# Attentions 0 and 2 of a four-layer cross-attention kernel: reciprocal, head sum and small TensorE pieces placed elsewhere in a half

## Chip, cores and metric

The kernel runs on one core of a Trainium2 chip. The metric is the time of one execution on the device in microseconds (us), as a median over runs.

## The reference

Four layers follow each other, and each adds a cross-attention and a feed-forward part to `x` (32 batches of 56 rows of 128 values). All four attentions look at the same context `ctx_768` (32 x 1500 x 96). Attentions 0 and 2 have 16 heads of 8 values:

```python
q = (einsum('bld,ed->ble', layernorm(x), Wq) + bq) -> (b, 56, 16, 8)
k, v = projections of ctx_768                       -> (b, 1500, 16, 8)
att = softmax(q . k / sqrt(8), over the 1500 keys)
x = x + (att . v) @ Wo + bo
```

Attention 2 has no biases and takes a mask of the keys. Attention 1 (heads of 64), attention 3 (one head) and the feed-forward parts are written by other code, which the change leaves alone.

## The kernel before

Everything is float32, the products of the projections in part as a high and a low float32r piece. Attentions 0 and 2 run `attend_turned`, each engine with a program of its own, tied by semaphores. The batches go in pairs. A pair is worked in four **halves** (h = 0 to 3; 64 halves for the 16 pairs): half h of pair i is batch 2i + h // 2 and heads 8 (h % 2) onwards. `pairs` writes out the halves at both ends and loops over those between. An order written out by hand decides everything: `half` of TensorE has twelve slots k = 0 to 11, and in slot k it issues

- `turned_scores`: two matmuls of scores with the keys on the partitions, into one of three PSUM buffers (`ring`); ScalarE's `exps` makes probabilities of them (`prob_t`). The order of uses of `ring` stands in `turns` (T is a slot, X the projection of a part of the keys or values), and each use waits for the reader of the use three before it;
- `scores`: one matmul of scores with the queries on the partitions for the half after the next one, into one of three banks (`ps_s`); VectorE's `maxima` takes their row maximum. Scores k waits for maximum k - 3.

Between the slots stand the smaller pieces: `keys` (odd halves, k = 0, 2, 4), whose result ScalarE's `high_keys` and VectorE's `low_keys` split into `k_hi` and `k_lo`, which the SyncE queue then copies into `ks` for the scores (`spread_keys`, six DMAs, eight with the mask row); `values` (even halves, k = 2, 4, 6); `products` (probabilities times values, three groups per half, two of them at k = 1 of the next half); `shifts` (turns the maxima, for `keep_shifts` on ScalarE); `queries`; `project`; and `denominators`, whose result VectorE's `invert` takes the reciprocal of. GpSimd picks queries by head (`pick_queries`), masks the sums by head (`own_rows`) and multiplies by the reciprocal (`quotient`). `ps_m` is one PSUM bank that shifts, queries, projection and denominators share in turn, so each waits for the reader of the one before.

The ring's order of use, for even and odd halves:

```python
turns = ("T0 T1 T2 X0 T3 T4 X1 T5 T6 X2 T7 T8 T9 T10 T11", "T0 X0 T1 T2 X1 T3 T4 X2 T5 T6 T7 T8 T9 T10 T11")
```

Of the kernel before, what the change touches and what calls it, by code (L numbers as in the profile page):

```python
# [29 lines left out]
ALU = mybir.AluOpType  # L30
ACT = mybir.ActivationFunctionType
AX = mybir.AxisListType
# [289 lines left out]
def attend_turned(nc, g, name, ctx_t, masked, ob, wk, wq3, bq3, wv, wo6):  # L322
# [16 lines left out]
    with ExitStack() as ctx:  # L339
# [21 lines left out]
         picked, scored, maxed, combined, max_high, max_split, shift_made, shifted, turned, exped, summed, o_kept,  # L361
         den_made, inverted, own_made, reduced, av_made, projected, out_kept) = (st.sem(x) for x in (
             "prepared", "filled", "k_made", "high_made", "k_kept", "v_made", "v_kept", "q_made", "q_biased",
             "q_rounded", "q_split", "picked", "scored", "maxed", "combined", "max_high", "max_split", "shift_made",
             "shifted", "turned", "exped", "summed", "o_kept", "den_made", "inverted", "own_made", "reduced",
             "av_made", "projected", "out_kept"))
# [10 lines left out]
        def asks(i, h):  # L377

            return h == (1 if isinstance(i, int) and i < 0 else 0) and among(i + 1, NP)
# [63 lines left out]
        def _(pool):  # L443
            def own_rows(m, b):

                pool.wait_ge(o_kept, m + 1)
                if up(m):
# [5 lines left out]
                    ALU.mult).then_inc(own_made, 1)  # L453

            def low_queries(i, h):

                pool.wait_ge(q_rounded, i + 2)
                if h == 0 and up(4 * i):
                    pool.wait_ge(own_made, 4 * i)
                low = slice(2 * qd, 3 * qd)  # L460
                pool.tensor_tensor(qp[low, :], qf[low, :], qp[low, :].bitcast(F32), ALU.subtract).then_inc(q_split, 1)
# [26 lines left out]
            def half(i, h):  # L488
# [5 lines left out]
                if among(m - 1, halves):  # L494
                    own_rows(m - 1, (h - 1) % 2)
                if asks(i, h):
                    low_queries(i, h)
# [13 lines left out]
        def _(pe):  # L511
# [145 lines left out]
            def half(i, h):  # L657
# [4 lines left out]
                for k in range(KT):  # L662
# [6 lines left out]
                    if k == 1 and behind:  # L669
                        products(m - 1, 2 * i + h // 2 - (1 - hf), (h - 1) % 4 // 2, (h - 1) % 2, 1)  # L670
                        products(m - 1, 2 * i + h // 2 - (1 - hf), (h - 1) % 4 // 2, (h - 1) % 2, 2)
                    if k == 1 and among(m + 1, halves):
                        shifts(i, h)
                    if x_live and not hf and k in (2, 4, 6):
                        values(i, h, k // 2 - 1)
                    if k == 5 and asks(i, h):
                        queries(i)
                    if k == (6 if hf else 7) and live:
                        products(m, n, h // 2, hf, 0)
                    if k == 7 and h == 1 and up(i):  # L680
                        project(i)
                    if k == 9 and behind:
                        denominators(i, h)
# [5 lines left out]
        def _(dve):  # L689
# [25 lines left out]

            def maxima(i, h, u):

                w = 4 * i + h + 2
                for c in range(BANKS):
                    dve.wait_ge(scored, 12 * w + 3 * u + c + 1)  # L720
                    dve.tensor_reduce(bank_max[:, h % 2, u, c:c + 1], ps_s[0:ur, c, 0:BK], AX.X, ALU.max  # L721
                                      ).then_inc(maxed, 1)

# [20 lines left out]

            def sum_heads(m):

                dve.wait_ge(own_made, m + 1)
                if up(m):
                    dve.wait_ge(av_made, m)
                dve.tensor_reduce(av_sum[:].rearrange("p (x l) -> p x l", x=groups),  # L750
                                  own_o[:].rearrange("p (x h l) -> p x l h", x=groups, h=3), AX.X, ALU.add
                                  ).then_inc(reduced, 1)

            def half(i, h):
                m, n, hf = 4 * i + h, 2 * i + h // 2, h % 2
                live, max_live = among(m - 1, halves), among(m + 2, halves)
                x_live = hf and among(n + 2, total)

                def unit(u):
                    if max_live:  # L760
                        maxima(i, h, u)

                if among(m - 2, halves):
                    invert(m - 2)
                if x_live:
                    low_keys(i, h, 0)
                unit(0)
                if x_live:
                    low_keys(i, h, 1)
                unit(1)  # L770
                if x_live:
                    low_keys(i, h, 2)
                if asks(i, h):
                    queries(i)
                if live:
                    sum_heads(m - 1)
                unit(2)
                unit(3)
                if max_live:
                    row_shifts(i, h)  # L780
# [26 lines left out]
        def _(act):  # L807
# [55 lines left out]
            def half(i, h):  # L863
# [11 lines left out]

                for k in range(7):
                    exps_of(k)
                    if k in ((0, 2, 4) if hf else (2, 4, 6)):
                        extra(k // 2 - (0 if hf else 1))
                    if k == 1 and among(m - 1, halves):  # L880
                        keep_sums(m - 1, (h - 1) % 2)
                    if k == 2 and among(m + 1, halves):
                        keep_shifts(i, h)
                if h == 1 and up(i):
                    out(i)
                exps_of(7, 8, 9, 10, 11)

# [1482 lines left out]
```

## Time and profile before

| | us |
|---|---|
| median of 3 runs | 5119.68 (5119.68 to 5135.09) |
| the profiled execution | 5126.65, its span 5125.0 |
| attention 0, first to last window | 204 to 1135 |
| attention 2 | 3660 to 4560 |
| rows of the page: PE, DVE, ACT, POOL busy | 4333.7, 3398.1, 2291.1, 1103.7 |

PE is TensorE's matmuls, DVE VectorE, ACT ScalarE, POOL GpSimd, SPq the DMA queue that SyncE issues. A row of a timeline is a run of like instructions: where it starts, how long it lasts, what it is, and in brackets how long its engine was idle ahead of it and for whom. Matmuls are pipelined, so the start of the next row, and not the length, tells what a piece costs.

### The profile page before, as it was taken

Reading aid. Unit: us, or ns where it says so; the run is one execution under the profiler, and the core shown is the slowest. Engines: PE = TensorE matmul, PEld = TensorE weight load, DVE = VectorE, ACT = ScalarE, POOL = GpSimd, SP = SyncE. Lnnn points to the kernel's source line nnn. Section 1 sums busy time; section 2 is a strip of 40 time slices with the busy share of each in tenths; the row PEclk is TensorE's granted clock in tenths of the full one; section 3 lists DMA queues with packets and bytes.
Section 4 is the critical chain, followed back from the end, with each engine's and each line's share of the span. In section 5 each row is a group of like instructions: output and inputs, shape, how many; then the busy total and the mean of one; then the engine's idle time right before and its main releaser. Section 6 shows DMA issues by size and latency. Waiting matters only on the chain. (4 is left out here: it accounts for less than half of the span.)

```text
span 5125.0 us, 100217 instructions
## 1 busy us (share of the span) xinstructions
PE 4333.7 (85%) x34185; PEld 3681.2 (72%) x34185; DVE 3398.1 (66%) x6401; ACT 2291.1 (45%) x4584; POOL 1103.7 (22%) x918
## 2 busy tenths in 40 slices
PE   5499999985599999999999667788699999969684
PEld 4277777764599899999999655566477777756573
DVE  4477777865666666665665466677677777755545
ACT  0066666652133333333333244465266666644341
POOL 0112221212101111111111044565122212213320
PEclk6599999987799999999999877888699999978897
DMA  7344445420101101101101100000245445410382
GB/s 244 91 109 108 102 105 112 103 47 10 46 19 33 24 19 33 24 19 33 24 19 24 43 25 0 0 0 0 64 108 113 103 101 113 108 30 16 71 181 46
DMA packets 190680, 316.83 MB, mean 62 GB/s; under 512 B 132372, under 2 KB 140870, under 8 KB 190406
## 3 DMA queue, kind: packets, MB, share of 16 engines
q1 hardware_dynamic: 186822, 294.71, 25.7%
q10 hardware_dynamic: 3584, 18.43, 0.9%
q8 instruction: 175, 2.87, 0.3%
q14 instruction: 99, 0.81, 0.1%
HBM read 146.07 MB, written 19.54 MB: 32 GB/s over the span
## 5 line engine op out<-in xcount | busy, mean ns | idle before, releaser
L1383 ACT ACTIVATE a1m_prob<-a1m_ps_s,a1m_neg_max 128x500 f32<-128x500 f32 x672 | 405.8, 675 | 588.7 <-DVE a1m_neg_max L1319 588.7
L1238 PE MATMUL a1m_ps_o<-a1m_cn,a1m_prob_t 125*128 125x97 f32 x5376 | 638.3, 276 | 0.2 <-issue 0.2
L1238 PEld LDWEIGHTS a1m_ps_o<-a1m_cn,a1m_prob_t 125*128 125x128 f32 x5376 | 624.7, 194 | 0.4 <-issue 0.4
L721 DVE TENSOR_REDUCE a0m_bank_max<-a0m_ps_s 112x1 f32<-112x500 f32 x768 | 486.7, 669 | 145.7 <-PE a0m_ps_s L583 140.6
L721 DVE TENSOR_REDUCE a2m_bank_max<-a2m_ps_s 112x1 f32<-112x500 f32 x768 | 486.4, 669 | 145.4 <-PE a2m_ps_s L583 140.5
L1316 DVE TENSOR_REDUCE a1m_bank_max<-a1m_ps_s 128x1 f32<-128x500 f32 x672 | 455.4, 678 | 174.1 <-PE a1m_ps_s L1204 172.7
L1204 PE MATMUL a1m_ps_s<-a1m_cxt,a1m_qhi 98*128 98x500 f32 x1344 | 442.3, 411 | 22.2 <-issue 18.1
L814 ACT ACTIVATE a0m_prob_t<-a0m_ring 125x448 f32<-125x448 f32 x768 | 385.9, 545 | 122.5 <-PE a0m_ring L537 115.3
L814 ACT ACTIVATE a2m_prob_t<-a2m_ring 125x448 f32<-125x448 f32 x768 | 386.0, 546 | 119.1 <-PE a2m_ring L537 111.7
L1220 PE MATMUL a1m_ps_t<-g_ident,a1m_prob 128*125 128x128 f32 x2688 | 378.2, 277 | 5.4 <-issue 4.3
L1220 PEld LDWEIGHTS a1m_ps_t<-g_ident,a1m_prob 128*125 128x125 f32 x2688 | 350.6, 190 | 26.4 <-issue 7.6
L1166 POOL TENSOR_TENSOR a1m_cxt<-a1m_raw,g_zeros 98x1500 fp32r<-98x1500 f32 x32 | 86.1, 2690 | 1297.3 <-PE a1m_ps_s L1204 1250.4
L537 PE MATMUL a0m_ring<-a0m_qs,a0m_ks 99*125 99x224 f32 x1536 | 357.0, 315 | 3.0 <-ACT a0m_prob_t L814 2.6
L537 PE MATMUL a2m_ring<-a2m_qs,a2m_ks 99*125 99x224 f32 x1536 | 355.8, 314 | 3.4 <-ACT a2m_prob_t L814 2.9
L583 PE MATMUL a2m_ps_s<-a2m_ks,a2m_qs 97*112 97x500 f32 x768 | 311.2, 409 | 23.5 <-DMA a2m_ks<-ctx_t 18.4
L583 PE MATMUL a0m_ps_s<-a0m_ks,a0m_qs 96*112 96x500 f32 x768 | 310.7, 408 | 22.9 <-DMA a0m_ks<-a0m_k_hi 17.9
L537 PEld LDWEIGHTS a0m_ring<-a0m_qs,a0m_ks 99*125 99x125 f32 x1536 | 264.7, 190 | 79.7 <-issue 35.4
L537 PEld LDWEIGHTS a2m_ring<-a2m_qs,a2m_ks 99*125 99x125 f32 x1536 | 264.0, 189 | 79.8 <-issue 35.2
L1327 DVE COPY a1m_prob_t<-a1m_ps_t 125x512 f32<-125x512 f32 x448 | 289.0, 686 | 8.0 <-PE a1m_ps_t L1220 7.0
L1391 ACT ACTIVATE a1m_prob_t<-a1m_ps_t 125x512 f32<-125x512 f32 x224 | 133.8, 597 | 357.1 <-PE a1m_ps_t L1220 357.1
L1204 PEld LDWEIGHTS a1m_ps_s<-a1m_cxt,a1m_qhi 98*128 98x128 f32 x1344 | 241.1, 193 | 59.8 <-issue 21.9
L1335 DVE RECIPROCAL a1m_den<-a1m_ps_o 128x1 f32<-128x1 f32 x224 | 37.7, 168 | 359.0 <-PE a1m_ps_o L1238 359.0
(783 smaller groups left out, 9138.8 us busy)
## 6 DMA issues: line engine op xcount, KB each, us to landing
a0m_ks<-a0m_k_hi SPq DMA_DIRECT2D x256, 187.5 KB
a2m_ks<-a2m_k_hi SPq DMA_DIRECT2D x256, 187.5 KB
a0m_ks<-a0m_k_lo SPq DMA_DIRECT2D x128, 187.5 KB
a2m_ks<-a2m_k_lo SPq DMA_DIRECT2D x128, 187.5 KB
ctx_t<-cprep_tr ACTq DMA_DIRECT2D x32, 562.5 KB
a0m_raw<-ctx_t SPq DMA_DIRECT2D x32, 562.5 KB
a1m_raw<-ctx_t SPq DMA_DIRECT2D x32, 562.5 KB
a2m_raw<-ctx_t SPq DMA_DIRECT2D x32, 562.5 KB
```

What stands on the lines that cost most here:

```text
L537: r = pe.matmul(out[0:NK, q * hr // 2:(q + 1) * hr // 2], ks[0:kt, b, x, k * NK:(k + 1) * NK], qs[0:kt, b, x * hr // 2:(x + 1) * hr // 2], ...
L583: r = pe.matmul(ps_s[0:ur, c, 0:BK], qs[0:kr, b, at:at + ur], ks[0:kr, b, x, c * BK:(c + 1) * BK], start=True, stop=True)
L721: dve.tensor_reduce(bank_max[:, h % 2, u, c:c + 1], ps_s[0:ur, c, 0:BK], AX.X, ALU.max).then_inc(maxed, 1)
L814: act.activation(prob_t[:, k // 4, k % 4, :], ring[where[h % 2, "T", k] % 3][0:NK, 0:hr], ACT.Exp).then_inc(exped, 1)
L1166: pool.tensor_tensor(cxt[:, h, 0, :], raw[:, h, :], g.zeros[0:CR, 0:1].broadcast_to([CR, S]), ALU.add).then_inc(high_made[h], 1)
L1204: m = pe.matmul(ps_s[:, k, 0:BK], part[:, b, h, at], cxt[:, h, w, keys], start=(part is qhi and w == 0 and h == sequences(u)[0]), stop=(pa ...
L1220: m = pe.transpose(ps_t[(BANKS * u + k) % 2][0:NK, q * P:(q + 1) * P], prob[:, u % 2, t * NK:(t + 1) * NK], g.ident[:])
L1238: m = pe.matmul(ps_o[at, 0:CO], prob_t[:, u % 2, t, at], cn[:, h, t, :], start=(t == 0), stop=(t == KT - 1))
L1316: dve.tensor_reduce(bank_max[:, s, k:k + 1], ps_s[:, k, 0:BK], AX.X, ALU.max).then_inc(bank_maxed, 1)
L1327: dve.tensor_copy(prob_t[:, u % 2, k * GT:(k + 1) * GT, :], ps_t[(BANKS * u + k) % 2][0:NK, :].rearrange("p (t r) -> p t r", t=GT)).then_i ...
L1383: act.activation(prob[:, s, k * BK:(k + 1) * BK], ps_s[:, k, 0:BK], ACT.Exp, bias=neg_max[:, s:s + 1]).then_inc(exped, 1)
L1391: act.activation(prob_t[:, u % 2, 2 * GT:KT, :], ps_t[(BANKS * u + 2) % 2][0:NK, :].rearrange("p (t r) -> p t r", t=GT), ACT.Copy).then_in ...
```

## The change

It touches `attend_turned` alone. (1) VectorE's reciprocal stands behind the first two maxima of the half, and behind the first `low_keys` in odd halves; the second and third `low_keys` stand behind three and five maxima (three and six before). (2) The sum over three head groups is no longer one VectorE reduction but two GpSimd additions behind `own_rows`. (3) On TensorE, shifts move from k = 1 to 5, queries from 5 to 7, the first products from 6 and 7 to 7 and 8, projection from 7 to 8, denominators from 9 to 10. (4) ScalarE's `keep_shifts` moves from behind exponential 2 to behind exponential 5, and `out` from behind 6 to behind 7.

```diff
@@ -452,11 +452,22 @@
                     own[:, 0:3].rearrange("p (x h l) -> p x h l", x=1, l=1).broadcast_to([P, groups, 3, L]),
                     ALU.mult).then_inc(own_made, 1)
 
+            def sum_heads(m):
+
+                if up(m):
+                    pool.wait_ge(av_made, m)
+                pool.wait_ge(own_made, m + 1)
+                mine = own_o[:].rearrange("p (x h l) -> p x h l", x=groups, h=3)
+                total_av = av_sum[:].rearrange("p (x l) -> p x l", x=groups)
+                pool.tensor_tensor(total_av, mine[:, :, 0, :], mine[:, :, 1, :], ALU.add).then_inc(paired, 1)
+                pool.wait_ge(paired, m + 1)
+                pool.tensor_tensor(total_av, total_av, mine[:, :, 2, :], ALU.add).then_inc(reduced, 1)
+
             def low_queries(i, h):
 
                 pool.wait_ge(q_rounded, i + 2)
                 if h == 0 and up(4 * i):
-                    pool.wait_ge(own_made, 4 * i)
+                    pool.wait_ge(reduced, 4 * i)
                 low = slice(2 * qd, 3 * qd)
                 pool.tensor_tensor(qp[low, :], qf[low, :], qp[low, :].bitcast(F32), ALU.subtract).then_inc(q_split, 1)
 
@@ -493,6 +504,7 @@
                     quotient(i, h)
                 if among(m - 1, halves):
                     own_rows(m - 1, (h - 1) % 2)
+                    sum_heads(m - 1)
                 if asks(i, h):
                     low_queries(i, h)
                 if isinstance(m, int) and m == -3:
@@ -669,17 +681,17 @@
                     if k == 1 and behind:
                         products(m - 1, 2 * i + h // 2 - (1 - hf), (h - 1) % 4 // 2, (h - 1) % 2, 1)
                         products(m - 1, 2 * i + h // 2 - (1 - hf), (h - 1) % 4 // 2, (h - 1) % 2, 2)
-                    if k == 1 and among(m + 1, halves):
+                    if k == 5 and among(m + 1, halves):
                         shifts(i, h)
                     if x_live and not hf and k in (2, 4, 6):
                         values(i, h, k // 2 - 1)
-                    if k == 5 and asks(i, h):
+                    if k == 7 and asks(i, h):
                         queries(i)
-                    if k == (6 if hf else 7) and live:
+                    if k == (7 if hf else 8) and live:
                         products(m, n, h // 2, hf, 0)
-                    if k == 7 and h == 1 and up(i):
+                    if k == 8 and h == 1 and up(i):
                         project(i)
-                    if k == 9 and behind:
+                    if k == 10 and behind:
                         denominators(i, h)
 
             pe.wait_ge(prepared, 1)
@@ -713,13 +725,11 @@
                 dve.tensor_tensor(k_lo[:, at], ring[where[1, "X", c] % 3][:, 0:BK], k_hi[:, at].bitcast(F32), ALU.subtract
                                   ).then_inc(k_kept, 1)
 
-            def maxima(i, h, u):
-
-                w = 4 * i + h + 2
-                for c in range(BANKS):
-                    dve.wait_ge(scored, 12 * w + 3 * u + c + 1)
-                    dve.tensor_reduce(bank_max[:, h % 2, u, c:c + 1], ps_s[0:ur, c, 0:BK], AX.X, ALU.max
-                                      ).then_inc(maxed, 1)
+            def maxima(i, h, u, c):
+
+                dve.wait_ge(scored, 12 * (4 * i + h + 2) + 3 * u + c + 1)
+                dve.tensor_reduce(bank_max[:, h % 2, u, c:c + 1], ps_s[0:ur, c, 0:BK], AX.X, ALU.max
+                                  ).then_inc(maxed, 1)
 
             def row_shifts(i, h):
 
@@ -742,40 +752,30 @@
                     dve.wait_ge(av_made, m)
                 dve.reciprocal(rec[:], ps_m[:, 0:gw]).then_inc(inverted, 1)
 
-            def sum_heads(m):
-
-                dve.wait_ge(own_made, m + 1)
-                if up(m):
-                    dve.wait_ge(av_made, m)
-                dve.tensor_reduce(av_sum[:].rearrange("p (x l) -> p x l", x=groups),
-                                  own_o[:].rearrange("p (x h l) -> p x l h", x=groups, h=3), AX.X, ALU.add
-                                  ).then_inc(reduced, 1)
-
             def half(i, h):
                 m, n, hf = 4 * i + h, 2 * i + h // 2, h % 2
-                live, max_live = among(m - 1, halves), among(m + 2, halves)
+                max_live = among(m + 2, halves)
                 x_live = hf and among(n + 2, total)
 
-                def unit(u):
-                    if max_live:
-                        maxima(i, h, u)
-
+                def banks(first, last):
+                    for k in range(first, last + 1) if max_live else ():
+                        maxima(i, h, k // BANKS, k % BANKS)
+
+                banks(0, 1)
+                if x_live:
+                    low_keys(i, h, 0)
                 if among(m - 2, halves):
                     invert(m - 2)
-                if x_live:
-                    low_keys(i, h, 0)
-                unit(0)
+                banks(2, 2)
                 if x_live:
                     low_keys(i, h, 1)
-                unit(1)
+                banks(3, 4)
                 if x_live:
                     low_keys(i, h, 2)
+                banks(5, 7)
                 if asks(i, h):
                     queries(i)
-                if live:
-                    sum_heads(m - 1)
-                unit(2)
-                unit(3)
+                banks(8, 11)
                 if max_live:
                     row_shifts(i, h)
 
@@ -873,17 +873,17 @@
                     for k in ks_ if live else ():
                         exps(i, h, k)
 
-                for k in range(7):
+                for k in range(8):
                     exps_of(k)
                     if k in ((0, 2, 4) if hf else (2, 4, 6)):
                         extra(k // 2 - (0 if hf else 1))
                     if k == 1 and among(m - 1, halves):
                         keep_sums(m - 1, (h - 1) % 2)
-                    if k == 2 and among(m + 1, halves):
+                    if k == 5 and among(m + 1, halves):
                         keep_shifts(i, h)
                 if h == 1 and up(i):
                     out(i)
-                exps_of(7, 8, 9, 10, 11)
+                exps_of(8, 9, 10, 11)
 
             pairs(act, half)
 
```

A hunk that only adds the semaphore `paired` is left out. VectorE in the odd half h = 3 of the first pair, before (the small reductions into `neg_max` and `shift` belong to the half ahead):

```order
L735 TENSOR_TENSOR a0m_shift<-a0m_neg_max,a0m_shift 112x4
L743 RECIPROCAL a0m_rec<-a0m_ps_m 128x168
L713 TENSOR_TENSOR a0m_k_lo<-a0m_ring,a0m_k_hi 128x500
L721 TENSOR_REDUCE a0m_bank_max<-a0m_ps_s 112x1 x3
L713 TENSOR_TENSOR a0m_k_lo<-a0m_ring,a0m_k_hi 128x500
L721 TENSOR_REDUCE a0m_bank_max<-a0m_ps_s 112x1 x3
L713 TENSOR_TENSOR a0m_k_lo<-a0m_ring,a0m_k_hi 128x500
L750 TENSOR_REDUCE a0m_av_sum<-a0m_own_o 128x168
L721 TENSOR_REDUCE a0m_bank_max<-a0m_ps_s 112x1 x6
L728 TENSOR_REDUCE a0m_neg_max<-a0m_bank_max 112x4
```

And with the change:

```order
L745 TENSOR_TENSOR a0m_shift<-a0m_neg_max,a0m_shift 112x4
L731 TENSOR_REDUCE a0m_bank_max<-a0m_ps_s 112x1 x2
L725 TENSOR_TENSOR a0m_k_lo<-a0m_ring,a0m_k_hi 128x500
L753 RECIPROCAL a0m_rec<-a0m_ps_m 128x168
L731 TENSOR_REDUCE a0m_bank_max<-a0m_ps_s 112x1
L725 TENSOR_TENSOR a0m_k_lo<-a0m_ring,a0m_k_hi 128x500
L731 TENSOR_REDUCE a0m_bank_max<-a0m_ps_s 112x1 x2
L725 TENSOR_TENSOR a0m_k_lo<-a0m_ring,a0m_k_hi 128x500
L731 TENSOR_REDUCE a0m_bank_max<-a0m_ps_s 112x1 x7
```

The reciprocal has gone behind two maxima and the first `k_lo`, the third `k_lo` has one maximum less ahead of it, and `av_sum` is gone.

TensorE in the same half from its first products on, before:

```order
L598 MATMUL a0m_ps_o<-a0m_prob_t,a0m_vals 32x112 x4
L633 MATMUL a0m_ps_m<-g_ident,a0m_shift 32x112 x4
L537 MATMUL a0m_ring<-a0m_qs,a0m_ks 125x224 x2
L583 MATMUL a0m_ps_s<-a0m_ks,a0m_qs 112x500
L552 MATMUL a0m_ring<-a0m_raw,a_wk 128x500
L537 MATMUL a0m_ring<-a0m_qs,a0m_ks 125x224 x2
L583 MATMUL a0m_ps_s<-a0m_ks,a0m_qs 112x500
L537 MATMUL a0m_ring<-a0m_qs,a0m_ks 125x224 x2
L583 MATMUL a0m_ps_s<-a0m_ks,a0m_qs 112x500
L552 MATMUL a0m_ring<-a0m_raw,a_wk 128x500
L537 MATMUL a0m_ring<-a0m_qs,a0m_ks 125x224 x2
L583 MATMUL a0m_ps_s<-a0m_ks,a0m_qs 112x500
```

And with the change, the same stretch:

```order
L610 MATMUL a0m_ps_o<-a0m_prob_t,a0m_vals 32x112 x4
L549 MATMUL a0m_ring<-a0m_qs,a0m_ks 125x224 x2
L595 MATMUL a0m_ps_s<-a0m_ks,a0m_qs 112x500
L564 MATMUL a0m_ring<-a0m_raw,a_wk 128x500
L549 MATMUL a0m_ring<-a0m_qs,a0m_ks 125x224 x2
L595 MATMUL a0m_ps_s<-a0m_ks,a0m_qs 112x500
L549 MATMUL a0m_ring<-a0m_qs,a0m_ks 125x224 x2
L595 MATMUL a0m_ps_s<-a0m_ks,a0m_qs 112x500
L564 MATMUL a0m_ring<-a0m_raw,a_wk 128x500
L549 MATMUL a0m_ring<-a0m_qs,a0m_ks 125x224 x2
L595 MATMUL a0m_ps_s<-a0m_ks,a0m_qs 112x500
L645 MATMUL a0m_ps_m<-g_ident,a0m_shift 32x112 x4
```

The four shift transposes into `ps_m` have left the place behind the products and stand behind the slot that follows the third key projection. A little later in the same half, before:

```order
L537 MATMUL a0m_ring<-a0m_qs,a0m_ks 125x224 x2
L583 MATMUL a0m_ps_s<-a0m_ks,a0m_qs 112x500
L598 MATMUL a0m_ps_o<-a0m_prob_t,a0m_vals 32x168 x8
L598 MATMUL a0m_ps_o<-a0m_prob_t,a0m_vals 32x112 x4
L537 MATMUL a0m_ring<-a0m_qs,a0m_ks 125x224 x2
L583 MATMUL a0m_ps_s<-a0m_ks,a0m_qs 112x500
```

And with the change, from the row behind the shifts:

```order
L549 MATMUL a0m_ring<-a0m_qs,a0m_ks 125x224 x2
L595 MATMUL a0m_ps_s<-a0m_ks,a0m_qs 112x500
L549 MATMUL a0m_ring<-a0m_qs,a0m_ks 125x224 x2
L595 MATMUL a0m_ps_s<-a0m_ks,a0m_qs 112x500
L610 MATMUL a0m_ps_o<-a0m_prob_t,a0m_vals 32x168 x8
L610 MATMUL a0m_ps_o<-a0m_prob_t,a0m_vals 32x112 x4
L549 MATMUL a0m_ring<-a0m_qs,a0m_ks 125x224 x2
```

The products (into `ps_o`) now stand behind the turned scores of slot 7 and not ahead of them.

## Rows read from the trace of the kernel before

**Rows 1.** Windows: busy us (instructions) of each engine, clock, DMA; attention 0.

```profile
204.00:1135.00 931.00, 866.63 (x8854) 691.84 (x8853) 707.32 (x1237) 561.38 (x1201) 184.46 (x212) 0.96 0.45 99
```

**Rows 2.** Waits of TensorE, attention 0: us in total, times, longest.

```profile
PE a0m_ps_s L583 <- DMA a0m_ks<-a0m_k_hi: 17.9, 14, 4.8
```

**Rows 3.** Waits of TensorE, attention 2: the same columns.

```profile
PE a2m_ps_s L583 <- DMA a2m_ks<-ctx_t: 18.4, 14, 4.8
```

**Rows 4.** Timeline of TensorE, odd half h = 3: start us, us, what, count.

```profile
899.43 1.73 PE L598 MATMUL a0m_ps_o<-a0m_prob_t,a0m_vals 125*32 125x168 f32 x48
901.10 0.56 PE L633 MATMUL a0m_ps_m<-g_ident,a0m_shift 112*32 112x112 f32 x4
901.42 0.46 PE L537 MATMUL a0m_ring<-a0m_qs,a0m_ks 99*125 99x224 f32 x2
...
901.95 1.00 PE L552 MATMUL a0m_ring<-a0m_raw,a_wk 97*128 97x500 f32 x2
...
904.35 1.11 PE L552 MATMUL a0m_ring<-a0m_raw,a_wk 97*128 97x500 f32 x2 [0.50 <-DVE a0m_k_lo L713]
...
905.95 0.39 PE L583 MATMUL a0m_ps_s<-a0m_ks,a0m_qs 96*112 96x500 f32 x1
906.27 0.97 PE L598 MATMUL a0m_ps_o<-a0m_prob_t,a0m_vals 125*32 125x168 f32 x24
907.25 0.48 PE L537 MATMUL a0m_ring<-a0m_qs,a0m_ks 99*125 99x224 f32 x2
...
910.32 0.39 PE L583 MATMUL a0m_ps_s<-a0m_ks,a0m_qs 96*112 96x500 f32 x1
910.54 0.38 PE L537 MATMUL a0m_ring<-a0m_qs,a0m_ks 99*125 99x224 f32 x2
911.93 0.48 PE L583 MATMUL a0m_ps_s<-a0m_ks,a0m_qs 96*112 96x500 f32 x1 [1.00 <-DMA a0m_ks<-a0m_k_hi]
```

**Rows 5.** Timeline of VectorE, the same odd half.

```profile
899.15 1.20 DVE L743 RECIPROCAL a0m_rec<-a0m_ps_m 128x168 f32<-128x168 f32 x1
900.27 0.62 DVE L713 TENSOR_TENSOR a0m_k_lo<-a0m_ring,a0m_k_hi 128x500 fp32r<-128x500 f32 x1
900.80 2.03 DVE L721 TENSOR_REDUCE a0m_bank_max<-a0m_ps_s 112x1 f32<-112x500 f32 x3
903.61 0.68 DVE L713 TENSOR_TENSOR a0m_k_lo<-a0m_ring,a0m_k_hi 128x500 fp32r<-128x500 f32 x1 [0.78 <-ACT a0m_k_hi L832]
...
906.53 0.67 DVE L713 TENSOR_TENSOR a0m_k_lo<-a0m_ring,a0m_k_hi 128x500 fp32r<-128x500 f32 x1
```

**Rows 6.** Timeline of ScalarE, the same odd half: the third high-key copy.

```profile
905.49 0.59 ACT L832 ACTIVATE a0m_k_hi<-a0m_ring 128x500 fp32r<-128x500 f32 x1 [0.35 <-PE a0m_ring L552]
```

**Rows 7.** Timeline of TensorE, even half h = 2.

```profile
885.74 1.73 PE L598 MATMUL a0m_ps_o<-a0m_prob_t,a0m_vals 125*32 125x168 f32 x48
887.65 0.54 PE L633 MATMUL a0m_ps_m<-g_ident,a0m_shift 112*32 112x112 f32 x4 [0.18 <-DVE a0m_rec L743]
...
890.35 1.14 PE L566 MATMUL a0m_ring<-a_wv,a0m_raw 97*125 97x128 f32 x8
891.47 0.48 PE L537 MATMUL a0m_ring<-a0m_qs,a0m_ks 99*125 99x224 f32 x2
...
892.47 1.13 PE L566 MATMUL a0m_ring<-a_wv,a0m_raw 97*125 97x128 f32 x8
893.36 0.46 PE L537 MATMUL a0m_ring<-a0m_qs,a0m_ks 99*125 99x224 f32 x2
```

**Rows 8.** Timeline of ScalarE, the same even half.

```profile
890.32 0.53 ACT L856 ACTIVATE a0m_qs<-a0m_ps_m 32x448 fp32r<-32x448 f32 x1
890.88 0.98 ACT L814 ACTIVATE a0m_prob_t<-a0m_ring 125x448 f32<-125x448 f32 x2
```

**Rows 9.** Timeline of GpSimd, the odd half of rows 4.

```profile
900.50 0.55 POOL L470 TENSOR_TENSOR a0m_av<-a0m_av_sum,a0m_rec 128x168 f32<-128x168 f32 x1 [1.94 <-DVE a0m_rec L743]
901.85 1.02 POOL L449 TENSOR_TENSOR a0m_own_o<-a0m_o_sb,a0m_own 128x504 f32<-128x504 f32 x1 [0.81 <-ACT a0m_o_sb L823]
```

More of the change, by code:

```diff
@@ L361, in attend_turned @@
          picked, scored, maxed, combined, max_high, max_split, shift_made, shifted, turned, exped, summed, o_kept,
-         den_made, inverted, own_made, reduced, av_made, projected, out_kept) = (st.sem(x) for x in (
+         den_made, inverted, own_made, paired, reduced, av_made, projected, out_kept) = (st.sem(x) for x in (
              "prepared", "filled", "k_made", "high_made", "k_kept", "v_made", "v_kept", "q_made", "q_biased",
              "q_rounded", "q_split", "picked", "scored", "maxed", "combined", "max_high", "max_split", "shift_made",
-             "shifted", "turned", "exped", "summed", "o_kept", "den_made", "inverted", "own_made", "reduced",
+             "shifted", "turned", "exped", "summed", "o_kept", "den_made", "inverted", "own_made", "paired", "reduced",
              "av_made", "projected", "out_kept"))
```

## Prediction

> **What bounds it now.** I read the windows first. In attention 0's window TensorE (PE) is busy 866.6 of 931 us, far more than VectorE (DVE, 707.3), ScalarE (561.4) or GpSimd (184.5) [rows 1]. So an instruction taken off DVE or put on GpSimd is worth nothing by itself; only time in which PE stands still, or changes over from one kind of work to another, counts. The waits of PE come next: the largest in attention 0 is that of score matmuls for a key DMA, 17.9 us in 14 waits, one of 4.8 among them, at the start; attention 2 has the same, 18.4 us [rows 2, 3]. That likeness is why I price one attention and take it twice. The timelines then give the place of each. The loop body is four halves (h = 0 to 3), passed 16 times per attention, peeled ends included. I take one odd half (h = 3) and one even half (h = 2). I write T for a turned-scores pair (L537), S for a score matmul (L583), K for a key projection (L552), V for a value projection (L566), P for products (L598), H for the shift transposes (L633), D for the denominators (L616).
>
> Between plain slots a piece starts 0.22 us after the one before (S at 910.32, T at 910.54). The T and S behind an H take 0.53 together (901.42 to 901.95), not 0.44, and an S ahead of a P 0.32 (905.95 to 906.27) and not 0.22 [rows 4]. So an H in a slot of its own, which like P has 32 rows of output, costs about 0.1 ahead and 0.09 behind, 0.19; I call such a T or S broken.
>
> **The change part by part.** All in us per loop of four halves, minus is gain.
>
> *Odd halves, first part.* H leaves its place between P and T. P to H was 1.67 (899.43 to 901.10), H to T 0.32 [rows 4]. P to T now takes the 1.67 (0.01 more at most). That is -0.31. K at c = 1 comes that much earlier. From there to K at c = 2 is a chain: 901.95 to 904.35, 2.40 us, K, ScalarE's `k_hi`, DVE's `k_lo`, K. DVE idled 0.78 us before the `k_lo` of 903.61 for want of `k_hi` [rows 4, 5], so the chain is PE and ScalarE, and moving H does not shorten it: the 0.50 of idle PE ahead of K stays. The reciprocal is now behind two maxima and the first `k_lo`. A maximum is 0.68 at most (three in 2.03), the first `k_lo` 0.62, the reciprocal 1.20 [rows 5]: from 899.15, where the reciprocal began, two maxima, `k_lo`, reciprocal and the third maximum end 1.36 + 0.62 + 1.20 + 0.68 = 3.9 later, at 903.0. The second `k_lo` can start no sooner than its `k_hi`, now 903.6 - 0.3 = 903.3. 0.3 of cover: nothing lost. The first `k_lo` ends at 901.1, K c = 1 wants it at 901.6: nothing either.
>
> *Odd halves, second part.* Call the issue of K c = 2 time 0 (904.35). Its `k_hi` ran from 1.14 to 1.73 [rows 6]; the third `k_lo` began only at 2.18 (906.53) and ended at 2.85 [rows 5], because maximum 5 stood ahead of it on DVE, which waits for an S that was just made. The change puts it behind maximum 4. It can start at 1.76 and end at 2.44: 0.41 earlier. The T of k = 7 reuses that ring buffer and waits for it. Before, P filled the time and T came at 2.90 (907.25); now P stands behind that T, and H (0.32 + 0.18) ahead: its turn comes at 2.90 - 0.98 - 0.10 + 0.50 = 2.3, the `k_lo` only at 2.49. So a short new wait of 0.2. Summed to the end of slot 8: before 2.90 + 0.54 (T, S, broken) + 0.44 = 3.88; now 2.49 + 0.23 + 0.32 + 0.90 (P without its 0.08 of waiting) + 0.52 = 4.46. That is +0.58, of which H's own move gave back 0.31 above. **h = 1: +0.27.**
>
> *The DMA wait.* In h = 3 this does not add up, since the next half's first S waits for a key DMA. T at 910.54, S only at 911.93, which is 4.73 us after the third `k_lo` ended at 907.20 [rows 4, 5]. The key copies are issued from `k_lo`'s end, so the landing moves with it: from time 0 it was 7.58 (911.93), and becomes 2.44 + 4.73 = 7.17. PE would be there at 6.40 + 0.58 = 6.98, so it still waits, 0.2 instead of 1.2. Gain 0.41 plus the 0.31 of the first part. **h = 3: -0.72.** (In h = 1 the matmuls of `project` stand in the way as well, and with 14 waits for 16 loops there is no room for a second one in a loop: no gain.)
>
> *Even halves.* ScalarE's copy of the shifts (890.32, 0.53) stands ahead of the exponentials that start at 890.88, and the T at 891.47 waits for the first of these [rows 8]: V to T took 1.12 (890.35 to 891.47) where the next V took 0.89 (892.47 to 893.36) [rows 7]. The copy moves behind exponential 5: -0.23 in both even halves. The value copy ahead of the next V also comes sooner; if that V of 0.89 waits for it, there is more to gain in h = 2, somewhere from 0 to another 0.2: I take -0.10. H of h = 2 waited for the reciprocal: P to H 1.91 (885.74 to 887.65) against 1.67 [rows 7, 4]: -0.24; in its new slot the reciprocal is long done. Against that H in a slot of its own and P with one more broken T, +0.19 each. **h = 0: -0.04, h = 2: -0.38.**
>
> *Heads summed by GpSimd.* DVE loses 0.72 per half, GpSimd gains two additions of 128x168; the same shape took it 0.55 (900.50) [rows 9], so 1.1 more in each half on an engine busy a fifth of the time. The next reader is the quotient a half later. Nothing. What is queued behind it, `low_queries`, feeds a pick a half away: nothing. Without this cover (if the sum were late for the quotient) the projection of h = 1 would wait, up to 1.1 per loop.
>
> *Queries, denominators, projection one to two slots later.* The same work in other slots; the broken T's are counted above. The projection's copy to `addt` now has one exponential ahead of it: nothing.
>
> **Sum.** -0.04 + 0.27 - 0.38 - 0.72 = -0.87 per loop. In 15 steady loops of each attention 13.0 us, in both 26. Profiled run: 5126.65 - 26 = 5100.6. That run was 7 above the median of 5119.68, so the median should be **5094**.
>
> **Bounds.** H's changeovers: 0 to 0.5 per half (0.5: S ahead of it takes its whole 0.39, +0.17, H its whole 0.56 and not 0.32, +0.24, and the T behind +0.09) [rows 4]. At 0 the even halves gain 0.38 a loop more (11 us over 30 loops), at 0.5, taken twice in even halves and half hidden in odd ones, about 0.9 less (28 us). The landing: if other transfers hold it and not `k_lo`, 0.41 x 30 = 12 us are lost.
> The Trainium skill (TensorEngine Tiling, Key Properties) says that a change of the tiling mode drains TensorE. H and P write 32 columns of the array, T and S do not. By a full drain S ahead of H would take its whole 0.39 us (the duration of the S at 905.95) and not the 0.32 of the row ahead of P: 0.07 a half, 9 us less gain over 128 halves. I stay with the row, which shows a changeover of that kind.
>
> **Rivals.**
> 1. *The forecast*, 62%: 5094, its own range 5080 to 5107.
> 2. *The changeovers eat it*, 20%: H in its own slot costs 0.5, or the landing does not follow `k_lo`. For: nothing in the rows shows an S ahead of an H. Against: P is the same size and costs 0.32. Time: 5094 + 12 to 28 = 5106 to 5122, about 5113. No change that can be measured.
> 3. *GpSimd and DVE get in each other's way*, 8%, the one that ends slower. The reciprocal comes about 2 us later, so the quotient and `own_rows` (1.02 us, 901.85) [rows 9] slide onto the second `k_lo` of an odd half. If one engine had to stand still for the other, that `k_lo` would be up to 0.7 late, K c = 2 too, 1.4 a loop, 42 us in all: 5094 + 42 = 5136. It decides from 0.7; under 0.2 it hides. Against: the `k_lo` of 900.27 ran beside the quotient of 900.50 and took 0.62, the shortest of its kind [rows 5, 9].
> The Trainium skill (SBUF — State Buffer, Who interferes with whom) has a shared port that blocks DVE when it reads two SBUF inputs; `k_lo` reads one from PSUM. By that rule there is no clash, and the row agrees.
> 4. *More than forecast*, 10%: H costs nothing apart and the `k_hi` chain gets faster too: 5094 - 18 = 5076.
>
> **Chances.** A difference of 0.3% (15 us) is about what a measurement of this kernel can tell from no change, so the bounds are 5104 and 5135. Most of the first rival (56 of 62) and all of the fourth lie under 5104, with 4 of the second: faster 0.70. The rest of these two, and some of the third: 0.22. Slower: 0.08. The range takes in the fourth rival and reaches the top of the second: 5070 to 5121.
>
> **What would show it.** In the profile after, the DMA wait of S falls from 17.9 to about 7 us (the first 4.8, and 0.2 a loop); the 0.50 of idle PE at K c = 2 stays; the T behind the third `k_lo` shows a new wait of 0.2; H waits for no reciprocal. Wrong would be: V to T still 1.12; the S wait still 1.0 with `k_lo` 0.4 earlier; S ahead of H over 0.45; a `k_lo` of over 0.8 us.

## The result

| | before | with the change |
|---|---|---|
| median of 7 runs each, us | 5119.68 | 5083.85 |
| ratio of the runs | 1 | 0.9931, 95% interval 0.9919 to 0.9943 |
| the profiled execution's span | 5125.0 | 5080.0 |
| POOL busy over the span | 1103.7 | 1238.1 |
| DVE busy over the span | 3398.1 | 3323.1 |

The change takes 36 us (0.7%) off; forecast were 26. The two profiled executions differ by 45. I looked for the place of that in the starts of the 48-fold products: in attention 0 the first to the last of them takes 847.3 us before and 829.1 after, in attention 2 846.2 and 827.2, and between the last of attention 0 and the first of attention 2, in code that did not change, lie 2581.8 and 2573.8. So 37 of the 45 us come from the two attentions, about as much as the medians say, and 8 are the spread of executions.

The windows of attention 0, the columns as in [rows 1]:

```profile
202.00:1110.00 908.00, 860.06 (x8855) 685.92 (x8854) 668.81 (x1177) 555.49 (x1200) 251.15 (x340) 0.97 0.46 102
```

TensorE (PE) is busy 860 us where it was 867, in a window that is 23 us shorter (its ends are rounded by hand; the products give 18). VectorE (DVE) lost 38 us of work, GpSimd gained 67.

The waits of TensorE in attention 0: the key projection K for `k_lo`, before and after, and the S for the key copies after the change ([rows 2] has it before):

```profile
PE a0m_ring L552 <- DVE a0m_k_lo L713: 24.2, 34, 6.3
PE a0m_ring L564 <- DVE a0m_k_lo L725: 25.8, 34, 6.4
PE a0m_ps_s L595 <- DMA a0m_ks<-a0m_k_hi: 4.7, 1, 4.7
```

The listed wait for the key copies fell from 17.9 us in 14 to the 4.7 at the start; what is left in each loop shows only in the start times below. The largest wait of TensorE was and is that of K for `k_lo`, and the change does not touch it.

TensorE in the odd half h = 3 and into the next half, the place of [rows 4] (T is now L549, S L595, K L564, P L610, H L645, V L578):

```profile
886.57 1.73 PE L610 MATMUL a0m_ps_o<-a0m_prob_t,a0m_vals 125*32 125x168 f32 x48
888.23 0.48 PE L549 MATMUL a0m_ring<-a0m_qs,a0m_ks 99*125 99x224 f32 x2
...
888.77 1.00 PE L564 MATMUL a0m_ring<-a0m_raw,a_wk 97*128 97x500 f32 x2
...
891.17 1.10 PE L564 MATMUL a0m_ring<-a0m_raw,a_wk 97*128 97x500 f32 x2 [0.50 <-DVE a0m_k_lo L725]
...
892.55 0.55 PE L645 MATMUL a0m_ps_m<-g_ident,a0m_shift 112*32 112x112 f32 x4
...
893.17 0.39 PE L595 MATMUL a0m_ps_s<-a0m_ks,a0m_qs 96*112 96x500 f32 x1
893.66 0.48 PE L549 MATMUL a0m_ring<-a0m_qs,a0m_ks 99*125 99x224 f32 x2
893.98 0.38 PE L595 MATMUL a0m_ps_s<-a0m_ks,a0m_qs 96*112 96x500 f32 x1
894.29 0.97 PE L610 MATMUL a0m_ps_o<-a0m_prob_t,a0m_vals 125*32 125x168 f32 x24
...
897.93 0.38 PE L549 MATMUL a0m_ring<-a0m_qs,a0m_ks 99*125 99x224 f32 x2
898.33 0.48 PE L595 MATMUL a0m_ps_s<-a0m_ks,a0m_qs 96*112 96x500 f32 x1
```

Between P (886.57) and T (888.23) no H stands any more, and P to the third K takes 4.60 (886.57 to 891.17) where it took 4.92 (899.43 to 904.35). The second K starts at 888.77 and the third at 891.17: 2.40 us, as before, with the same 0.50 of idle PE. Then three things that the forecast named. H stands in a slot of its own at 892.55. T of slot 7 waits: S at 893.17, T at 893.66, 0.49 where a plain one takes 0.22. And the first S of the next half comes 0.40 after its T (897.93, 898.33), where [rows 4] had 1.39. Counted from K, that S is at 7.16, before at 7.58; forecast was 7.17.

VectorE in the same half, the place of [rows 5]:

```profile
887.35 0.67 DVE L725 TENSOR_TENSOR a0m_k_lo<-a0m_ring,a0m_k_hi 128x500 fp32r<-128x500 f32 x1
887.93 1.20 DVE L753 RECIPROCAL a0m_rec<-a0m_ps_m 128x168 f32<-128x168 f32 x1
...
890.43 0.68 DVE L725 TENSOR_TENSOR a0m_k_lo<-a0m_ring,a0m_k_hi 128x500 fp32r<-128x500 f32 x1 [0.77 <-ACT a0m_k_hi L832]
...
892.93 0.68 DVE L725 TENSOR_TENSOR a0m_k_lo<-a0m_ring,a0m_k_hi 128x500 fp32r<-128x500 f32 x1 [0.65 <-ACT a0m_k_hi L832]
```

GpSimd in the same stretch, the place of [rows 9]:

```profile
889.77 1.03 POOL L449 TENSOR_TENSOR a0m_own_o<-a0m_o_sb,a0m_own 128x504 f32<-128x504 f32 x1
890.94 0.54 POOL L462 TENSOR_TENSOR a0m_av_sum<-a0m_own_o 128x168 f32<-128x168 f32 x1
891.55 0.54 POOL L464 TENSOR_TENSOR a0m_av_sum<-a0m_av_sum,a0m_own_o 128x168 f32<-128x168 f32 x1
```

The third `k_lo` (892.93) waits for ScalarE's `k_hi` and no longer for a maximum, and ends 2.44 after K's 891.17. The second (890.43) ran beside the last 0.37 us of `own_rows` (889.77 to 890.80) and the start of the first addition, and took 0.68; the third, with GpSimd idle (its last row here ends at 892.09), took 0.68.

TensorE in an even half (h = 0), the place of [rows 7]:

```profile
903.25 1.14 PE L578 MATMUL a0m_ring<-a_wv,a0m_raw 97*125 97x128 f32 x8
904.15 0.46 PE L549 MATMUL a0m_ring<-a0m_qs,a0m_ks 99*125 99x224 f32 x2
904.45 0.39 PE L595 MATMUL a0m_ps_s<-a0m_ks,a0m_qs 96*112 96x500 f32 x1
904.68 0.55 PE L645 MATMUL a0m_ps_m<-g_ident,a0m_shift 112*32 112x112 f32 x4
904.99 0.46 PE L549 MATMUL a0m_ring<-a0m_qs,a0m_ks 99*125 99x224 f32 x2
```

ScalarE in the same half, the place of [rows 8]:

```profile
902.93 0.27 ACT L847 ACTIVATE a0m_vals<-a0m_ring 125x128 f32<-125x128 f32 x1
903.08 0.99 ACT L814 ACTIVATE a0m_prob_t<-a0m_ring 125x448 f32<-125x448 f32 x2
...
905.55 0.53 ACT L856 ACTIVATE a0m_qs<-a0m_ps_m 32x448 fp32r<-32x448 f32 x1
```

The median of V to T at this place is 0.90 (here 903.25 to 904.15), not 1.12: the exponentials at 903.08 follow the value copy directly, the copy of the shifts comes at 905.55. H has no wait. And S to H is 0.23 (904.45 to 904.68): no premium ahead of H at all, where I had put 0.1.

All later readings rest on one measure, the time from the start of one 48-fold P to the next, which is one half. Medians over the 15 or 16 passes of attention 0, in us; the last column is 32 times the difference of the sums, for 16 loops in each of two attentions:

| kernel | h = 1 | h = 2 | h = 3 | h = 0 | sum | x 32 |
|---|---|---|---|---|---|---|
| before | 13.32 | 13.70 | 13.32 | 14.13 | 54.47 | |
| changed | 13.67 | 13.19 | 12.60 | 13.98 | 53.44 | -33 |
| third `k_lo` behind maximum 5 | 14.09 | 13.20 | 13.01 | 13.98 | 54.28 | -6 |
| reciprocal first | 13.68 | 13.20 | 12.61 | 13.98 | 53.47 | -32 |
| sum on VectorE | 13.68 | 13.20 | 12.60 | 13.98 | 53.46 | -32 |
| VectorE's order alone | 14.50 | 14.90 | 14.08 | 14.98 | 58.46 | +128 |
| before, `k_lo` ahead of 5 | 13.22 | 13.70 | 12.94 | 14.20 | 54.06 | -13 |
| H in slot 3, P in slot 6 | 12.93 | 13.20 | 12.58 | 13.98 | 52.69 | -57 |
| early copies, changed | 13.67 | 13.20 | 12.33 | 13.99 | 53.19 | -41 |
| early copies, before | 13.31 | 13.70 | 12.21 | 14.75 | 53.97 | -16 |
| both of these | 12.91 | 13.20 | 11.91 | 13.98 | 52.00 | -79 |
| even halves back | 13.68 | 13.57 | 12.61 | 14.57 | 54.43 | -1 |

### The profile page after: what moved, and what is told of

Same layout as the page of the kernel before. It is cut to its first block and busy times, and to the rows that moved or that the text cites. A ratio compares the mean times of both kernels' runs of the same rounds, so it can differ in the third digit from the quotient of the medians.

```text
span 5080.0 us, 100345 instructions
## 1 busy us (share of the span) xinstructions
PE 4317.0 (85%) x34185; PEld 3663.3 (72%) x34185; DVE 3323.1 (65%) x6273; ACT 2280.0 (45%) x4584; POOL 1238.1 (24%) x1174
## 3 DMA queue, kind: packets, MB, share of 16 engines
q1 hardware_dynamic: 186822, 294.71, 25.8%
## 5 line engine op out<-in xcount | busy, mean ns | idle before, releaser
L549 PE MATMUL a0m_ring<-a0m_qs,a0m_ks 99*125 99x224 f32 x1536 | 365.4, 320 | 5.5 <-ACT a0m_prob_t L814 2.2
L549 PE MATMUL a2m_ring<-a2m_qs,a2m_ks 99*125 99x224 f32 x1536 | 363.8, 319 | 5.5 <-ACT a2m_prob_t L814 2.2
L549 PEld LDWEIGHTS a0m_ring<-a0m_qs,a0m_ks 99*125 99x125 f32 x1536 | 257.3, 189 | 90.8 <-issue 63.3
L549 PEld LDWEIGHTS a2m_ring<-a2m_qs,a2m_ks 99*125 99x125 f32 x1536 | 256.4, 188 | 90.2 <-issue 63.0
L595 PE MATMUL a2m_ps_s<-a2m_ks,a2m_qs 97*112 97x500 f32 x768 | 308.5, 405 | 7.0 <-DMA a2m_ks<-ctx_t 4.8
L595 PE MATMUL a0m_ps_s<-a0m_ks,a0m_qs 96*112 96x500 f32 x768 | 306.7, 402 | 7.5 <-DMA a0m_ks<-a0m_k_hi 4.7
```

The source lines that it names most:

```text
L549: r = pe.matmul(out[0:NK, q * hr // 2:(q + 1) * hr // 2], ks[0:kt, b, x, k * NK:(k + 1) * NK], qs[0:kt, b, x * hr // 2:(x + 1) * hr // 2], ...
L595: r = pe.matmul(ps_s[0:ur, c, 0:BK], qs[0:kr, b, at:at + ur], ks[0:kr, b, x, c * BK:(c + 1) * BK], start=True, stop=True)
```

## The experiments

Each was timed beside the kernel before on the same chip; ratios are to that kernel. The changed kernel stands at 0.9931. The first four and the next four shared a chip each, as did the last two. "Against the changed kernel" means the difference of the two ratios, times 5117 us. By the intervals such a difference is known to 8 to 13 us either way, so for smaller effects the table of halves decides.

**Third `k_lo` behind maximum 5 again.**

```diff
-                banks(3, 4)
+                banks(3, 5)
                 if x_live:
                     low_keys(i, h, 2)
-                banks(5, 7)
+                banks(6, 7)
```

> The changed kernel with one thing undone: the third k_lo of an odd half stands behind maximum 5 again, not behind maximum 4. My theory (the key landing and the T of slot 7 both hang on the end of that k_lo): both come 0.4 us later in each odd half, 0.8 a loop, some 31 loops: +25 us against the changed kernel, so near 5109, and the S at the start of h = 0 waits about 0.6 and not 0.2. Rival (the landing is held by other transfers, VectorE's order is indifferent): no more than +12 us.

Measured: 5110.34 us, ratio 0.9984 (0.9971 to 0.9997), 27 us above the changed kernel. The odd halves are 0.42 and 0.41 longer in the table, the even ones unchanged. VectorE of this kernel in h = 3:

```profile
911.15 0.68 DVE L731 TENSOR_REDUCE a0m_bank_max<-a0m_ps_s 112x1 f32<-112x500 f32 x1 [0.47 <-PE a0m_ps_s L595]
911.74 0.67 DVE L725 TENSOR_TENSOR a0m_k_lo<-a0m_ring,a0m_k_hi 128x500 fp32r<-128x500 f32 x1
```

TensorE there:

```profile
909.56 1.10 PE L564 MATMUL a0m_ring<-a0m_raw,a_wk 97*128 97x500 f32 x2 [0.50 <-DVE a0m_k_lo L725]
...
911.56 0.40 PE L595 MATMUL a0m_ps_s<-a0m_ks,a0m_qs 96*112 96x500 f32 x1
912.47 0.48 PE L549 MATMUL a0m_ring<-a0m_qs,a0m_ks 99*125 99x224 f32 x2 [0.51 <-DVE a0m_k_lo L725]
```

The maximum at 911.15 holds the `k_lo` to 911.74, and the T comes 2.91 after K, as before the change, but now with nothing in front of it: 0.51 us of idle PE. My theory had one slip: the first S of the next half waits no longer than in the changed kernel (T to S 0.41 on the median against 0.40), since PE and the landing shift by the same 0.4. The cost is the same. The rival is out: time follows `k_lo`.

**Reciprocal first.**

```diff
-                banks(0, 1)
-                if x_live:
-                    low_keys(i, h, 0)
                 if among(m - 2, halves):
                     invert(m - 2)
-                banks(2, 2)
+                if x_live:
+                    low_keys(i, h, 0)
+                banks(0, 2)
```

> The changed kernel with the reciprocal at the head of the half again (reciprocal, first k_lo, three maxima). Theory: with the shifts in slot 5 nobody waits for the reciprocal or for the first maxima, so its place is worth nothing: within 3 us of the changed kernel (5084). Rival (the reciprocal ahead of maxima and k_lo was itself the cost): +10 us or more.

Measured: 5085.27 us, ratio 0.9937 (0.9915 to 0.9959). That is 3 us above the changed kernel. The intervals alone would leave room for the rival's 10; the table does not, since its row is that of the changed kernel to 0.01, 1 us in all. The part of the change that the title names first is worth nothing that shows here.

**Sum over heads on VectorE again** (GpSimd's `sum_heads` taken out, the old reduction behind `queries`).

```diff
...
                 if asks(i, h):
                     queries(i)
+                if live:
+                    sum_heads(m - 1)
                 banks(8, 11)
```

> The changed kernel with the sum over heads back on VectorE as one reduction, behind the queries. Theory: VectorE is not what TensorE waits for, so 0 to +3 us against the changed kernel. Rival A (the relief of VectorE is part of the gain): +8 us or more. Rival B (GpSimd's additions disturb VectorE): faster than the changed kernel.

Measured: 5088.17 us, ratio 0.9944 (0.9927 to 0.9961), 7 us above the changed kernel (4 by the medians), and the intervals overlap. No half is longer by more than 0.01, which speaks against rival A. One small loss is at the end of each attention, where the last reciprocal stands behind the reduction: the last `project` waits 2.5 us for GpSimd's quotient and 2.0 in the changed kernel, 1 us in all. The rest has no place in the trace of attention 0 and may be noise.

**VectorE's order without the rest** (TensorE's and ScalarE's orders as before).

```diff
-                    if k == 5 and among(m + 1, halves):
+                    if k == 1 and among(m + 1, halves):
                         shifts(i, h)
-                    if k == 7 and asks(i, h):
+                    if k == 5 and asks(i, h):
                         queries(i)
-                    if k == (7 if hf else 8) and live:
+                    if k == (6 if hf else 7) and live:
                         products(m, n, h // 2, hf, 0)
...
```

> The changed kernel with TensorE's and ScalarE's orders as before the change; VectorE's order and GpSimd's sum stay. Theory: the shifts of slot 1 need the shared PSUM bank that the reciprocal frees, and the reciprocal is now 1.9 to 3 us into the half: each half waits about 1 us, 3.7 a loop net of the earlier landing, +115 us against the kernel before, near 5235. Rival (each part brings its share by itself): faster than the kernel before.

Measured: 5236.81 us, ratio 1.0226 (1.0202 to 1.0250), +116 us against the kernel before. The wait of TensorE for the reciprocal in attention 0, from the view of waits (sum in us, count, longest):

```profile
PE a0m_ps_m L645 <- DVE a0m_rec L753: 65.4, 60, 1.4
```

One of them on TensorE's timeline:

```profile
580.80 1.73 PE L610 MATMUL a0m_ps_o<-a0m_prob_t,a0m_vals 125*32 125x168 f32 x48
583.92 0.54 PE L645 MATMUL a0m_ps_m<-g_ident,a0m_shift 112*32 112x112 f32 x4 [1.39 <-DVE a0m_rec L753]
```

VectorE beside it:

```profile
581.39 1.26 DVE L731 TENSOR_REDUCE a0m_bank_max<-a0m_ps_s 112x1 f32<-112x500 f32 x2
582.58 1.20 DVE L753 RECIPROCAL a0m_rec<-a0m_ps_m 128x168 f32<-128x168 f32 x1
```

H is ready behind P, and the bank that it writes is freed by the reciprocal, which ends at 583.78. 60 waits of 1.1 us on average. VectorE's new order (with GpSimd's sum, which costs nothing inside a half) is a loss of 2.3% unless the shifts go to a later slot.

**The kernel before with the third `k_lo` ahead of maximum 5, alone.**

```diff
...
-                unit(1)
+                for c in range(BANKS - 1) if max_live else ():
+                    maxima(i, h, 1, c)
                 if x_live:
                     low_keys(i, h, 2)
+                if max_live:
+                    maxima(i, h, 1, BANKS - 1)
```

> The kernel before with one edit: the third k_lo of an odd half goes ahead of maximum 5. Theory: the key copies start and land 0.4 us sooner, which comes off the wait of the first S of h = 0, and about 0.08 off the T behind the products: 0.49 a loop, 31 loops, -15 us against the kernel before, near 5104. Rival (the landing is held by other transfers): -3 us or less.

Measured: 5102.49 us, ratio 0.9973 (0.9964 to 0.9982), -14 us against the kernel before. h = 3 is 0.38 shorter, h = 1 0.10, and h = 0 0.07 longer: with less waiting for keys, its H begins to wait for the reciprocal.

**Shifts in slot 3 and products in slot 6 of odd halves.**

```diff
-                    if k == 5 and among(m + 1, halves):
+                    if k == (3 if hf else 5) and among(m + 1, halves):
                         shifts(i, h)
...
-                    if k == (7 if hf else 8) and live:
+                    if k == (6 if hf else 8) and live:
                         products(m, n, h // 2, hf, 0)
...
-                    if k == 5 and among(m + 1, halves):
+                    if k == (3 if hf else 5) and among(m + 1, halves):
                         keep_shifts(i, h)
```

> The changed kernel, odd halves only: shifts (with their copy) in slot 3 and the first products in slot 6 again. Theory: between the second and third key projection TensorE stands still 0.5 us for k_lo, so the shifts cost nothing there, and the products fill the wait of T for the third k_lo: h = 1 loses 0.7, h = 3 only 0.2, since its end hangs on the key landing. 0.9 a loop, -28 us against the changed kernel, near 5056. Rival (the chain from projection to projection gets longer by the copy of the shifts on ScalarE): no gain.

Measured: 5061.45 us, ratio 0.9892 (0.9877 to 0.9907), 20 us below the changed kernel (22 by the medians, 24 by the table). The timing does not tell that from the expected 28; the halves show where it falls short. TensorE of h = 1:

```profile
858.12 1.00 PE L564 MATMUL a0m_ring<-a0m_raw,a_wk 97*128 97x500 f32 x2
...
859.42 0.55 PE L645 MATMUL a0m_ps_m<-g_ident,a0m_shift 112*32 112x112 f32 x4
859.73 0.46 PE L549 MATMUL a0m_ring<-a0m_qs,a0m_ks 99*125 99x224 f32 x2
...
860.52 1.11 PE L564 MATMUL a0m_ring<-a0m_raw,a_wk 97*128 97x500 f32 x2
...
862.45 0.97 PE L610 MATMUL a0m_ps_o<-a0m_prob_t,a0m_vals 125*32 125x168 f32 x24
863.35 0.48 PE L549 MATMUL a0m_ring<-a0m_qs,a0m_ks 99*125 99x224 f32 x2
```

K to K is still 2.40 (858.12 to 860.52) with H in between, so H is free; P comes ahead of the T at 863.35, which does not wait. h = 1 is 0.74 shorter as expected, h = 3 by 0.02 and not by 0.2: its end hangs on the landing alone, and what PE saves it waits for (T to the first S of h = 0 is 1.14 on the median, 0.40 in the changed kernel). Two things moved together here, H and P, and no run moves one alone. TensorE's wait of K for `k_lo` in attention 0 falls from 25.8 to 9.7 us, since H and the T behind it now stand in that gap.

**The first head group's `k_hi` copies issued early**, in the changed kernel and in the one before.

```diff
-                    sp.wait_ge(k_kept, BANKS * (n + 1))
+                    kept = BANKS * (n + 1)
+                    sp.wait_ge(high_made, kept)
...
+                copies(2 * hf, (0, 2))
+                sp.wait_ge(k_kept, kept)
+                copies(2 * hf, (1,))
...
```

> The changed kernel; the SyncE queue issues the two k_hi copies of the first head group as soon as k_hi is there, and only the k_lo copy waits for k_lo. Theory: the keys land over 1 us earlier, and the 0.2 us wait at the start of h = 0 goes: -6 us against the changed kernel. Rival (the wait there is something else): 0.

> The kernel before with the same early k_hi copies and nothing else. Theory: the wait of 1.15 us at the start of h = 0 goes altogether: about -33 us against the kernel before, near 5086, as much as the whole change. Rival (the landing is held by the rate of the transfers and not by when they are issued): under half of that.

Measured: in the changed kernel 5078.20 us, ratio 0.9931 (0.9917 to 0.9944). Its ratio is that of the changed kernel; h = 3 is 0.27 shorter in the profile, but the timing doesn't tell this from nothing. In the kernel before: 5093.31 us, ratio 0.9959 (0.9945 to 0.9973), -21 us against the kernel before (-23 by the medians) and not -33. TensorE of the latter, from the end of h = 3:

```profile
523.18 0.38 PE L544 MATMUL a0m_ring<-a0m_qs,a0m_ks 99*125 99x224 f32 x2
523.44 0.47 PE L590 MATMUL a0m_ps_s<-a0m_ks,a0m_qs 96*112 96x500 f32 x1
...
524.28 1.73 PE L605 MATMUL a0m_ps_o<-a0m_prob_t,a0m_vals 125*32 125x168 f32 x48
526.61 0.54 PE L640 MATMUL a0m_ps_m<-g_ident,a0m_shift 112*32 112x112 f32 x4 [0.60 <-DVE a0m_rec L750]
```

VectorE there:

```profile
525.26 1.21 DVE L750 RECIPROCAL a0m_rec<-a0m_ps_m 128x168 f32<-128x168 f32 x1 [0.45 <-issue]
```

The 1.1 us wait of S (523.18 to 523.44) is gone, and H of h = 0 now waits 0.60 for the reciprocal of 525.26. The key wait had covered it. So the rival named the wrong cause, though its size (under half) would fit the table's 16 us: the landing does follow the issue, and another wait took its place. In h = 0 of the kernel before the reciprocal counts only once that cover is gone. With the reciprocal first and H in slot 5, above, no such wait appears: it is H's place, not the reciprocal's, that keeps it away.

**Both of these edits in the changed kernel.**

> The changed kernel with both further edits: shifts in slot 3 and first products in slot 6 of odd halves, and the first head group's k_hi copies issued as soon as k_hi is there. Theory: with the keys there in time, the 0.74 us that the first edit gave in h = 1 come in h = 3 too, and the 0.2 us wait there goes: 1.7 a loop, 31 loops, -50 us against the changed kernel, near 5034, ratio to the kernel before 0.983. Rival (as the early copies alone showed in the kernel before, something behind the wait was covered by it and now waits itself): a ratio of 0.987 or more.

Measured: 5036.67 us, ratio 0.9850 (0.9836 to 0.9864), 41 us below the changed kernel (47 by the medians, 46 by the table), the fastest of all. h = 3 is 0.69 shorter than in the changed kernel. Of the expected 1.7 a loop 1.44 came: PE reaches the first S of h = 0 sooner than in the kernel with the early copies alone, and there waits again (T to S 0.45 on the median, plain 0.22).

**Even halves back.**

```diff
-                    if k == 5 and among(m + 1, halves):
+                    if k == (5 if hf else 1) and among(m + 1, halves):
                         shifts(i, h)
...
+                if not hf and among(m - 2, halves):
+                    invert(m - 2)
                 banks(0, 1)
                 if x_live:
                     low_keys(i, h, 0)
-                if among(m - 2, halves):
+                if hf and among(m - 2, halves):
                     invert(m - 2)
...
```

> The changed kernel with even halves as before the change in two things: shifts in slot 1 with their copy behind exponential 2, and the reciprocal at the head of the half; odd halves stay. Theory: V to T is 1.12 again in both even halves, the shifts of h = 2 wait for the reciprocal, and the shifts of h = 0 now wait for it too, since the key wait no longer covers it: 0.15 + 0.5 + up to 0.6 a loop, +20 to +37 us against the changed kernel. Rival (even halves do not matter, the gain is all in the key landing): within 5 us.

Measured: 5111.35 us, ratio 0.9997 (0.9987 to 1.0008). That is +34 us against the changed kernel (+28 by the medians, +32 by the table): h = 2 is 0.38 longer, h = 0 0.59 longer. Without its part in the even halves the change gains nothing that can be measured. Part of that is again a wait uncovered: P to H of h = 0 takes 2.02 on the median, where the kernel before has 1.66, because the keys now come nearly in time and the reciprocal does not.

## Why the prediction was right, and where it was off

*The way and the place.* Idle PE at one S, removed by an earlier `k_lo`; shown by two experiments that move this `k_lo` alone, in opposite directions: -14 us in the kernel before, +27 in the changed one. The landing at 7.17 from K was measured at 7.16, the T of slot 7 at 2.49 was measured at 2.49.

*h = 3: -0.72 forecast, -0.72 measured.* Both terms came: P to the third K 0.32 less, the landing from there 0.42 less.

*h = 1: +0.27 forecast, +0.35 measured.* The size of one term: behind the waiting T I put a plain 0.23 to its S, and it took 0.32 (893.66 to 893.98). A T that waited is broken too. This miss goes against the two below, so the sum of a loop (-0.87 forecast, -1.03 measured) is nearer than its terms; that much was luck.

*h = 0 and h = 2: -0.04 and -0.38 forecast, -0.15 and -0.51 measured.* The terms for V to T (0.23), for the value copy (0.10) and for the reciprocal's wait (0.24) were right. Mis-sized was H in its own slot, with 0.19: ahead of it there is nothing (S to H 0.23), the T behind costs 0.08 more (T to S 0.30 on the median, plain 0.22). I had read the premium off an S ahead of a P, because both write 32 columns. The Trainium skill's rule on changes of the tiling mode (TensorEngine Tiling, Key Properties) would have made it larger still; no drain shows at this place, where H starts 0.23 after an S whose row lasts 0.39, and the measurement decides.

*The count.* I took 15 loops of each attention, it is 16, and left out the ends. 32 x 1.03 is 33 us, and the last `project` of each attention waits 0.5 less. With the forecast's own terms 16 loops would have given 28.

*A reading that was wrong.* The prediction calls the S's wait for the key copies the largest of TensorE. It was not: K waited 24.2 us for `k_lo` in 34 waits (one of the 0.50 stands in [rows 4]). Even without the longest wait of each kind, at the start, K's come to 17.9 and S's to 13.1. The forecast did not suffer, since it rightly left that gap as it is. But it is the larger room, and H in slot 3 of odd halves uses it.

*The rivals.* The changeovers did not eat it, and the landing follows `k_lo`. GpSimd and VectorE did not get in each other's way: the very overlap that I named took place, `k_lo` beside `own_rows`, at 0.68 us against 0.68, which also fits the rule of the Trainium skill (SBUF — State Buffer, Who interferes with whom). The fourth rival (5076) was near in size in part for another reason, cheaper changeovers, and not by a faster chain: K to K stayed 2.40.

*What the parts are worth.* The reciprocal's new place and GpSimd's sum are worth nothing that was measured inside a half. The gain is H and its copy in a later slot in even halves, and one maximum less ahead of the third `k_lo` in odd ones; in h = 3 another 0.32 comes from H leaving the place ahead of the second K, which no run moves alone. Odd halves as the change has them are not the best order: with P ahead of T again and H in the gap ahead of the third K the kernel is 20 us faster. What each of the two moves gives is not shown.

## What to carry to other kernels

An engine that is busy 93 to 95% of a stage can still be bound by waits of half a microsecond that recur; measure the start-to-start times of its pieces by position in the loop, and price a move by what stands in the gap that it leaves and in the one that it fills. A wait covers other waits: taking away one of 1.15 us gave 0.5, since a reciprocal behind it came to light, so look at what is late next. And when producer and consumer share a buffer in turn, moving the reader later is a loss (here 116 us) until the next writer is moved too.

## What the hardware showed that I had not expected

Four transposes with 32 rows of output cost nothing ahead of them behind a 500-column matmul (0.23 us start to start, plain 0.22 to 0.23), while products of the same 32 rows cost 0.32. Why these two differ stays open: the products also wait on exponentials and write four column positions, and no run separates the two. A T that had waited for its operand took 0.32 and not 0.22 to the next start (893.66 to 893.98), and an S that had waited 0.31 (the S of 911.93 before the change, and the median there). Why is open too.
